# Token means of the first phase by column-tiled float32 products instead of a centring product on every image

## The chip, the cores and the metric

One NeuronCore of a Trainium2 chip runs the whole program. The metric is device time in microseconds (us), the median of several executions. Engines: PE is TensorE, PEld its weight loads, DVE VectorE, ACT ScalarE, POOL GpSimd, SP the engine that issues most DMAs.

## What is computed

The input `x` has 32 images of 128 channels and 56x56 = 3136 tokens. The reference, cut to what matters:

```python
def _ln_c(v, eps=1e-06):
    m = jnp.mean(v, axis=1, keepdims=True)
    s = jnp.var(v, axis=1, keepdims=True)
    return (v - m) / jnp.sqrt(s + eps)

xa = sign_a(x)                # _L0_conv_ref, on _ln_c(x)
wq = quant_weight_W2(w)       # sign of centred, clipped weights, times alpha
y = conv_general_dilated(xa, wq, padding 1, 3x3) + b
mean, var = over (0, 2, 3)    # batch norm over all images
y = relu((y - mean) * rsqrt(var + EPS) * gamma + beta)

x = x + _L0_conv_ref(_ln_c(x), ...)
t = _to_tokens(x)
t = t + _L0_ffn_ref(_ln_t(t), ...)   # router, top half of the tokens, gelu FFN
x = _from_tokens(t, x)
```

Only the sign of the layer-normed input enters the convolution, and the divisor is positive: so the first phase needs sign(x - m), with m the mean over the 128 channels (the partitions) of each token. Batch norm needs the convolution of all 32 images before anything else can go on, hence two phases.

## The kernel before

Channels lie on the 128 partitions, tokens in the free dimension. An image is worked in NCH = 7 chunks of T = 448 tokens (8 rows of 56). **Phase 1** takes each image n through the convolution and stores it as f16 in DRAM (`y_int`); **phase 2** loads x and y again and does the rest (norm, router, search for the threshold, FFN), by tables of positions. The change touches phase 1 alone.

In phase 1 every engine has its own function `phase1(n, b)`, and the next image is made ready while this one is convolved:

- DVE (`split`, L581, and `split_low`, L585): for each chunk of image n+1 a rounded float32r copy `xh` and the rest `xl = x - xh`, into a ring of RING = 4 buffers each. Then `batch_stats` (L605): the statistics of a chunk of y of image n.
- PE (`centre`, L879 and L880): two float32r products of `centre_r` = identity - 1/128 with `xh` and `xl` into one of four PSUM banks: x - m, for one chunk. `newly_due(c)` says which chunks of image n+1 are centred behind which chunk of image n: 2 behind chunks 1, 3, 5 and 1 behind chunk 6. `conv` (L889): nine bf16 products, one for each tap, of a chunk, into one of two PSUM banks; it waits for `y_copied` of two chunks earlier, and for `signed` of its own image, one chunk ahead.
- ACT (`sign`, L479): the sign of the centred bank into the padded bf16 image `sg` (two of them, inside `yo`). L494: y of a chunk from PSUM to `y16`.
- SP: L354 loads image n+2 into `xb[b]` (1568 KB) once image n is split (`split_ready`), L359 stores y of image n (784 KB).

Loops of the engines run two images a turn. In phase 2, `router` (L942) makes a weighted sum over the 128 channels of each token by column-tiled products: 32 output partitions each, four chunks side by side in the four column quarters of the array, then three. The row goes by `wrow` (L753) and DRAM (`w_row`, L390) to `wse` (L395). The gate row comes back from DRAM onto 128 partitions as `gate_all` (L539). The FFN's second product (L986) has float32 operands: four for each chunk.

```python
for i, (w, t) in enumerate(((wsel_h, th), (wsel_h, tl), (wsel_l, th))):
    for q, c in enumerate(chunks):
        last = M(ps[q * COLS:(q + 1) * COLS, T_BANK, 0:T], w[:, COLS - part:2 * COLS - part], cut(t, c),
```

Of the kernel before, what the change touches and what calls it, by code (L numbers as in the profile page):

```python
# [16 lines left out]
C = 128  # L17
# [28 lines left out]
K_ID, K_CEN, K_STRI, K_TRIU, K_ONES, K_CAND, K_CIDX, K_MHALF, K_END = (  # L46
    0, 128, 256, 384, 416, 544, 560, 561, 561 + NT)


def constants():  # L50
# [10 lines left out]
    t[:, K_MHALF:K_END] = -0.5  # L61
# [21 lines left out]
def block_kernel(nc, consts, x_in, cw_in, cb_in, gamma_in, beta_in, wr_in, br_in, w1_in, b1_in,  # L83
# [10 lines left out]
    g_dram = nc.dram_tensor("gate_row", [n_img, TOK], f32).ap()  # L94
    w_dram = nc.dram_tensor("w_row", [n_img, TOK], f32).ap()

    with ExitStack() as ctx:
# [73 lines left out]
        wrow = sb("wrow", [C, T], f32)  # L171
        wse = sb("wse", [C, SLEN], f32)
# [13 lines left out]
        CEN_BANKS, CONV_BANK = (0, 1, 4, 5), 2  # L186
# [24 lines left out]
        x_in_s = [sem(f"x_in{b}") for b in range(2)]  # L211
# [70 lines left out]
        def newly_due(c):  # L282

            return (c - 1, c) if c % 2 else (c,) if c == NCH - 1 else ()

        def ring_free(n, c):

            if c >= RING:
                return n * NCH + c - RING + 1
            return (n - 1) * NCH + (c + RING if c + RING < NCH else c) + 1  # L290
# [28 lines left out]

        MASK_STEPS = 5  # L320
        PART = (slice(0, HALF * T), slice(HALF * T, TOK))
        P1 = (1, n_img - 1)
# [6 lines left out]
        def _(sp):  # L329
# [3 lines left out]
            sp.dma_start(xb[1][:, :], x_v[C:2 * C, :]).then_inc(x_in_s[1], 16)  # L333
            sp.dma_start(w1_f, w1_in).then_inc(params_in, 16)
# [77 lines left out]
        def _(pool):  # L412
# [27 lines left out]
            def phase2(n, b):  # L440
                for pos in range(POS):
                    for m, mb, _ in due(VAR_AT + 1, 1, n, b, pos):
                        pool.wait_ge(var_ready, m + 1)
                        nc.gpsimd.tensor_tensor(rm[:, 0, :], stw[:, 5, :], kt[0:TILE, K_MHALF:K_END],  # L444
                                                ALU.pow).then_inc(rstd_ready, 1)
# [14 lines left out]
        def _(act):  # L460
# [26 lines left out]
            def phase1(n, b):  # L487
                for c in range(NCH):
# [70 lines left out]
        def _(dve):  # L559
# [13 lines left out]
            def split(n, b, c):  # L573

                if is_int(n) and n == 0:
                    if c in (0, HALF):
                        dve.wait_ge(x_in_s[0] if c else x0_begun, 16)
                elif c == 0:
                    dve.wait_ge(x_in_s[b], (n - b) * 8 + 16)
                wait_count(dve, centred, ring_free(n, c))  # L580
                V.tensor_copy(xh[c % RING][:, :], cut(xb[b], c)).then_inc(xh_ready, 1)  # L581

            def split_low(n, b, c):
                dve.wait_ge(xh_ready, n * NCH + c + 1)
                V.tensor_tensor(xl[c % RING][:, :], cut(xb[b], c), xh[c % RING][:, :].bitcast(f32),  # L585
# [12 lines left out]
            for c in range(NCH):  # L598
                split(0, 0, c)
                split_low(0, 0, c)  # L600
# [6 lines left out]
            def phase1(n, b):  # L607
# [18 lines left out]
            phase1(1, 1)  # L626

            dve.wait_ge(squares_summed, 1)
            link(V.tensor_scalar(norms[:, :], ps[:, BC0, 0:2], float(C), 1e-30, ALU.mult, ALU.add))
# [432 lines left out]
```

## Time and profile before

| | us |
|---|---|
| runs: lowest, median, highest of 3 | 2133.52, 2137.33, 2137.93 |
| the profiled execution, its own time | 2127.27 |
| its span in the trace | 2125.5 |
| phase 1, to the end of image 31's convolutions | about 500 |
| PE busy over the span | 1994.1 (94%) |
| DVE, ACT, POOL busy | 1666.4, 1211.1, 933.1 |
| granted TensorE clock, mean | 0.987 |

A program prints the profile. In its rows "L986" is line 986 of the kernel before, "out<-in" are the program's names without buffer numbers, "x1792" is a count, and the text behind "<-" in brackets is what ended the engine's idle time. Records of matmuls overlap, since the array is pipelined: where matters of rate are concerned, starts are compared, not durations.

### The profile page before, as it was taken

To read this page: it belongs to the slowest core of one execution; us is meant where nothing else is said; L and a number is where in the kernel's file an instruction comes from. 1 tells how busy PE (TensorE), PEld (TensorE's weight loads), DVE (VectorE), ACT (ScalarE), POOL (GpSimd) and SP (SyncE) were. 2 spreads that over 40 slices of the span, in tenths; PEclk is the share of its full clock that TensorE was granted. 3 is DMA by queue.
4 is the path that set the end of the run, shared out by engine and by line. 5 is a ranking of instruction groups with operands and counts; after the bars stand their busy time and mean duration, and the time that the engine had idled before them with its cause. 6 is when DMAs were issued, how large, how long until landed. Compare 5 with 4: busy or idle time off the path is not lost. (4 is left out here: it accounts for less than half of the span.)

```text
span 2125.5 us, 35828 instructions
## 1 busy us (share of the span) xinstructions
PE 1994.1 (94%) x9515; PEld 1021.8 (48%) x9515; DVE 1666.4 (78%) x4766; ACT 1211.1 (57%) x2030; POOL 933.1 (44%) x714
## 2 busy tenths in 40 slices
PE   7999999995899999999999999999999999999995
PEld 4555555552444444444444444444444444444442
DVE  6777777775688888877788888888877888888875
ACT  4444444443656566666666666666666656666652
POOL 1000000003455556655556565556655656565543
PEclk9999999997899999999999999999999999999998
DMA  4434344443123332333333333333333333333213
GB/s 163 178 140 181 142 176 154 163 162 111 51 102 122 131 119 111 126 127 112 112 128 117 124 115 124 114 134 111 127 125 112 125 120 129 111 124 124 99 69 124
DMA packets 68726, 267.91 MB, mean 126 GB/s; under 512 B 22352, under 2 KB 27184, under 8 KB 64688
## 3 DMA queue, kind: packets, MB, share of 16 engines
q1 hardware_dynamic: 55264, 214.90, 27.5%
q10 hardware_dynamic: 13392, 52.29, 6.6%
q14 instruction: 52, 0.43, 0.1%
q8 instruction: 18, 0.29, 0.1%
HBM read 188.08 MB, written 77.87 MB: 125 GB/s over the span
## 5 line engine op out<-in xcount | busy, mean ns | idle before, releaser
L986 PE MATMUL ps<-hs,w_c 128*128 128x448 f32 x1792 | 763.7, 553 | 0.6 <-ACT yo L527 0.6
L517 ACT ACTIVATE hs<-ps,b1c,undo 128x448 f32<-128x448 f32 x896 | 609.2, 718 | 127.2 <-PE ps L977 123.4
L986 PEld LDWEIGHTS ps<-hs,w_c 128*128 128x128 f32 x1792 | 313.4, 190 | 208.6 <-issue 176.9
L889 PE MATMUL ps<-yo,cwT 128*128 128x448 bf16 x2016 | 408.7, 355 | 0.0
L430 POOL TENSOR_TENSOR tl<-tr,th 128x448 f16<-128x448 f32 x224 | 244.0, 1090 | 310.5 <-PE ps L977 192.9
L425 POOL TENSOR_TENSOR xb<-xb,zr 128x448 f32<-128x448 f32 x224 | 261.3, 1168 | 269.2 <-ACT zr L545 267.8
L975 PE MATMUL ps<-th,w_h 128*128 128x448 f16 x896 | 319.2, 356 | 19.8 <-ACT hs L517 19.7
L976 PE MATMUL ps<-tl,w_h 128*128 128x448 f16 x896 | 317.1, 354 | 0.0
L977 PE MATMUL ps<-th,w_l 128*128 128x448 f16 x896 | 317.0, 354 | 0.0
L437 POOL TENSOR_TENSOR yo<-yo,base 128x448 f32<-128x448 f32 x224 | 277.7, 1247 | 77.8 <-DVE yo L823 77.8
L527 ACT ACTIVATE yo<-ps,cols 128x448 f32<-128x448 f32 x224 | 141.5, 632 | 241.7 <-PE ps L986 241.4
L889 PEld LDWEIGHTS ps<-yo,cwT 128*128 128x128 bf16 x2016 | 185.9, 97 | 193.5 <-issue 24.3
L494 ACT ACTIVATE y<-ps 128x448 f16<-128x448 f32 x224 | 121.6, 543 | 258.9 <-PE ps L889 258.9
L545 ACT ACTIVATE zr<-y,bn_t,bn_s 128x448 f32<-128x448 f16 x224 | 169.2, 756 | 144.0 <-DMA y<-y_int 128.6
L605 DVE BATCH_NORM_STATS2 base<-y 128x448 f16 (+1 forms) x224 | 140.2, 627 | 118.5 <-ACT y L494 109.0
L729 DVE TENSOR_TENSOR ur<-xb,ps 128x448 f32<-128x448 f32 x224 | 138.5, 618 | 107.5 <-PE ps L966 100.6
L691 DVE BATCH_NORM_STATS2 st<-ps 112x6 f32<-112x128 f32 x896 | 195.1, 282 | 14.3 <-PE ps L931 10.3
L823 DVE TENSOR_TENSOR yo<-yo,gate_all 128x448 f32<-128x448 f32 x224 | 198.0, 887 | 7.9 <-DMA gate_all<-gate_row 7.9
L421 POOL TENSOR_TENSOR sm<-sm,kt 128x1 f32<-128x1 f32 x1 | 0.6, 564 | 452.3 <-DVE sm L679 452.3
L552 ACT ACTIVATE th<-tr 128x448 f16<-128x448 f32 x224 | 129.0, 576 | 106.3 <-DVE tr L738 91.9
L746 DVE SCALAR_TENSOR_TENSOR base<-tr,xb 128x448 f32<-128x448 f32 x224 | 186.7, 834 | 1.2
L444 POOL TENSOR_TENSOR rm<-stw,kt 112x28 f32<-112x28 f32 x32 | 153.5, 4797 | 34.4 <-DVE stw L709 34.4
(132 smaller groups left out, 2324.2 us busy)
## 6 DMA issues: line engine op xcount, KB each, us to landing
xb<-x SPq DMA_DIRECT2D x31, 1568.0 KB, 7.6
xb<-x SPq DMA_DIRECT2D x33, 896.0 KB, 4.5
gate_all<-gate_row ACTq DMA_DIRECT2D x32, 896.0 KB, 4.3
result<-yo SPq DMA_DIRECT2D x32, 896.0 KB, 3.5
y_int<-y SPq DMA_DIRECT2D x32, 784.0 KB, 3.6
xb<-x SPq DMA_DIRECT2D x33, 672.0 KB, 4.3
gate_all<-gate_row ACTq DMA_DIRECT2D x32, 672.0 KB, 5.5
result<-yo SPq DMA_DIRECT2D x32, 672.0 KB, 3.0
```

The lines of the kernel that those rows point to most:

```text
L425: nc.gpsimd.tensor_tensor(cut(xb[b], c), cut(xb[b], c), zr[(b + c) % 2][:, :], ALU.add).then_inc(x1_ready, 1)
L430: nc.gpsimd.tensor_tensor(cut(tl, c), tr[(b + c) % 2][:, :], cut(th, c), ALU.subtract).then_inc(tl_ready, 1)
L437: nc.gpsimd.tensor_tensor(cut(yo[b], c), cut(yo[b], c), cut(base[b], c), ALU.add).then_inc(out_ready, 1)
L517: nc.scalar.activation(hs[(b + slot) % 2][:, j, :], ps[:, H_BANK + j, 0:T], ACT.Gelu_apprx_tanh, bias=b1c[:, j:j + 1], scale=undo[:, 1:2]) ...
L691: last = V.bn_stats(st[:, c * TPG + i, :], ps[0:TILE, BC0 + c % 2, i * C:(i + 1) * C])
L746: V.scalar_tensor_tensor(cut(base[b], c), tr[ring][:, :], 1.0 / T_SCALE, cut(xb[b], c), ALU.mult, ALU.add).then_inc(base_ready, 1)
L823: V.tensor_tensor(cut(yo[b], c), cut(yo[b], c), cut(gate_all, c), ALU.mult).then_inc(gated, 1)
L889: last = M(bank, cwT[:, t, :], sg[b][:, c * ROWS + dy:c * ROWS + dy + ROWS, dx:dx + SIDE], start=t == 0, stop=t == TAPS - 1)
L975: M(bank, w1_h[:, blk], cut(th, c), start=True, stop=False)
L976: M(bank, w1_h[:, blk], cut(tl, c), start=False, stop=False)
L977: M(bank, w1_l[:, blk], cut(th, c), start=False, stop=True).then_inc(h_done, 1)
L986: last = M(bank, w2_c[:, j, :], hs[(b + c) % 2][:, j, :], start=first, stop=final)
```

## The change

- A third x buffer: `xs = [xb[0], xb[1], base[1]]`, image n in `xs[n % 3]`. What lay in `base[1]` (sign and absolute value of the weights, `w1_f`) goes to `th` and `tl`.
- Image 0 keeps the old way. For images 1 to 31, `token_means` on PE makes seven float32 products of a 128x32 stationary tile (one column of 1/128, the others zero) with chunks 0 to 3, then 4 to 6, of x: as in `router`, the four column quarters take a chunk each. For image n+2 it stands behind chunk 1 (`MEAN_SLOT`) of image n's convolution; image 1's stands behind chunk 0 of image 0.
- `copy_mean` on DVE copies the bank to `mrow` (which is `wrow`), behind the third `level` of its image slot. SP writes the seven rows to DRAM (`m_dram`) with two DMAs, waits for them, and reads the row back onto 128 partitions with two DMAs (896 and 672 KB): into `gate_all` for even images, `hs` for odd ones.
- `level` on DVE subtracts the mean in place in x, for one chunk of image n+1 at a time, in place of `split` and `split_low`. ACT takes the sign from there (SBUF), one chunk behind each y copy.
- The loops of PE, DVE and ACT run six images a turn; SP's is written out.
- The table of constants has 64 more columns; the load of image 2 stands ahead of the small parameters.

The diff, cut to its core:

```diff
     t[:, K_CIDX] = np.arange(C) % CAND
-    t[:, K_MHALF:K_END] = -0.5
+    t[:, K_MHALF:K_MSEL] = -0.5
+    t[:, K_MSEL + COLS] = 1.0 / C
     return t
...
 
         cw, cwc = (o[:, TOK - C * TAPS:TOK] for o in yo)
-        cwa = base[1][:, 0:C * TAPS]
-        cws = base[1][:, C * TAPS:C * TAPS * 3 // 2].bitcast(bf16).rearrange("o (t i) -> o t i", i=C)
-        w1_f = base[1][:, 2 * C * TAPS:2 * C * TAPS + HID]
+        cwa = th[:, 0:2 * C * TAPS].bitcast(f32)
+        cws = tl[:, 0:C * TAPS].bitcast(bf16).rearrange("o (t i) -> o t i", i=C)
+        w1_f = tl[:, C * TAPS:C * TAPS + 2 * HID].bitcast(f32)
+        xs = [xb[0], xb[1], base[1]]
...
+        mrow = wrow
...
-        CEN_BANKS, CONV_BANK = (0, 1, 4, 5), 2
+        CEN_BANKS, CONV_BANK, MEAN_BANK = (0, 1, 4, 5), 2, 6
...
+        def mean_part(b, part):
+
+            count = (HALF, NCH - HALF)[part]
+            if b == 0:
+                return gate_all[:, PART[part]]
+            return hs[part][:, 0:count, :].rearrange("p c t -> p (c t)")
+
+        def mean_cut(b, c):
+
+            return hs[c // HALF][:, c % HALF, :] if b else cut(gate_all, c)
...
+        MEAN_SLOT = 1
...
+            sp.dma_start(xs[2][:, :], x_v[2 * C:3 * C, :]).then_inc(x_in_s[2], 16)
...
 
-            def phase1(n, b):
-                sp.wait_ge(split_ready, (n + 1) * NCH)
+            def save_mean(m, b):
+                sp.wait_ge(mean_copied, m)
+                for part in range(2):
+                    count = min(NQ, NCH - part * NQ)
+                    sp.dma_start(m_dram[bass.ds(m, 1), part * NQ * T:(part * NQ + count) * T]
+                                 .rearrange("a (c t) -> (a c) t", t=T),
+                                 mrow[part:part + (count - 1) * COLS + 1:COLS, :]).then_inc(mean_saved, 16)
+                sp.wait_ge(mean_saved, m * 32)
+                if has(m - 2, 1):
+                    sp.wait_ge(levelled, (m - 2) * NCH)
+                for part in range(2):
+                    sp.dma_start(mean_part(b, part), m_dram[bass.ds(m, 1), PART[part]]
+                                 .to_broadcast([C, (HALF, NCH - HALF)[part] * T])).then_inc(mean_in[b][part], 16)
+
+            def phase1(n, i, k):
+                if has(n + 3):
+                    sp.wait_ge(signed, (n + 1) * NCH)
+                    sp.dma_start(xs[i % 3][:, :], x_v[bass.ds((n + 3) * C, C), :]).then_inc(x_in_s[i % 3], 16)
+                elif n + 2 >= n_img:
+                    sp.wait_ge(signed, (n + 1) * NCH)
+                    for part in range(2):
+                        load_x(n + 2 - n_img, n + 2 - n_img, part)
                 if has(n + 2):
-                    sp.dma_start(xb[b][:, :], x_v[bass.ds((n + 2) * C, C), :]).then_inc(x_in_s[b], 16)
-                else:
-                    for part in range(2):
-                        load_x(n + 2 - n_img, b, part)
+                    save_mean(n + 2, i % 2)
                 sp.wait_ge(y_copied, (n + 1) * NCH)
-                sp.dma_start(y_dram[bass.ds(n * C, C), :], y16[b][:, :]).then_inc(y_saved[b], 16)
-
-            pairs(sp, phase1, 1, n_img - 2, 0, n_img)
+                sp.dma_start(y_dram[bass.ds(n * C, C), :], y16[i % 2][:, :]).then_inc(y_saved[i % 2], 16)
+
+            save_mean(1, 1)
+            for n in range(n_img):
+                phase1(n, n % 6, n // 6)
...
-            def sign(n, b, c):
-                g = n * NCH + c
-                act.wait_ge(centred, g + 1)
+            def sign(m, i, c):
+                b = i % 2
+                if is_int(m) and m == 0:
+                    act.wait_ge(centred, c + 1)
+                    z = ps[:, CEN_BANKS[c % RING], 0:T]
+                else:
+                    act.wait_ge(levelled, (m - 1) * NCH + c + 1)
+                    z = cut(xs[i % 3], c)
                 if c == 0:
-                    if has(n - 2):
-                        act.wait_ge(conv_done, (n - 1) * NCH)
-                    if is_int(n) and n < 2:
-                        act.wait_ge(border_clear, n + 1)
-                bank = CEN_BANKS[c % RING]
+                    if has(m - 2):
+                        act.wait_ge(conv_done, (m - 1) * NCH)
+                    if is_int(m) and m < 2:
+                        act.wait_ge(border_clear, m + 1)
                 nc.scalar.activation(sg[b][:, 1 + c * ROWS:1 + (c + 1) * ROWS, 1:1 + SIDE],
-                                     ps[:, bank, 0:T].rearrange("p (r w) -> p r w", w=SIDE),
+                                     z.rearrange("p (r w) -> p r w", w=SIDE),
                                      ACT.Sign).then_inc(signed, 1)
 
             for c in range(RING):
                 sign(0, 0, c)
             nc.scalar.activation(cwa, cwc, ACT.Abs, accum_out=abs_sum).then_inc(abs_summed, 1)
 
-            def phase1(n, b):
+            def phase1(n, i, k):
+                b = i % 2
                 for c in range(NCH):
                     act.wait_ge(conv_done, n * NCH + c + 1)
                     if c == 0 and has(n - 2):
 
                         act.wait_ge(y_saved[b], (n - b) * 8)
                         act.wait_ge(bn_taken, (n - 1) * NCH)
-                    nc.scalar.activation(cut(y16[b], c), ps[:, CONV_BANK + (b + c) % 2, 0:T],
+                    nc.scalar.activation(cut(y16[b], c), ps[:, CONV_BANK + (i + c) % 2, 0:T],
                                          ACT.Copy).then_inc(y_copied, 1)
                     if is_int(n) and n == 0 and c < 2:
-                        for k in (range(RING, NCH - 1), range(NCH - 1, NCH))[c]:
-                            sign(0, 0, k)
+                        for q in (range(RING, NCH - 1), range(NCH - 1, NCH))[c]:
+                            sign(0, 0, q)
                     if has(n + 1):
-                        for k in newly_due(c):
-                            sign(n + 1, 1 - b, k)
-
-            pairs(act, phase1, 3, n_img - 1, 0, n_img)
+                        sign(n + 1, (i + 1) % 6, c)
+
+            sixes(act, phase1, 0, n_img, 1)
...
+            def copy_mean(m, b):
+                dve.wait_ge(mean_done, m)
+                if has(m - 1, 1):
+                    dve.wait_ge(mean_saved, (m - 1) * 32)
+                V.tensor_copy(mrow[:, :], ps[:, MEAN_BANK + b, 0:T]).then_inc(mean_copied, 1)
+
+            def level(m, i, k, c):
+
+                if c in (0, HALF):
+                    dve.wait_ge(mean_in[i % 2][c // HALF], k * 48 + (i + i % 2) * 8)
+                x_c = cut(xs[i % 3], c)
+                V.tensor_tensor(x_c, x_c, mean_cut(i % 2, c), ALU.subtract).then_inc(levelled, 1)
+
+            def phase1(n, i, k):
                 for c in range(NCH):
                     if has(n + 1):
-                        split(n + 1, 1 - b, c)
-                        split_low(n + 1, 1 - b, c)
+                        level(*image_after(1, n, i, k), c)
+                    if c == MEAN_SLOT + 1 and has(n + 2):
+                        copy_mean(n + 2, i % 2)
                     if c:
-                        batch_stats(n, b, c - 1)
+                        batch_stats(n, i % 2, c - 1)
                     elif has(n - 1):
-                        batch_stats(n - 1, 1 - b, NCH - 1)
-
-            phase1(0, 0)
+                        batch_stats(n - 1, (i + 1) % 2, NCH - 1)
...
+            def token_means(m, i, k):
+
+                b = i % 2
+                pe.wait_ge(x_in_s[i % 3], k * 32 + (i // 3) * 16 + 16)
+                if has(m - 2, 1):
+                    pe.wait_ge(mean_copied, m - 2)
+                for part in range(2):
+                    chunks = range(part * NQ, min(NCH, (part + 1) * NQ))
+                    for q, c in enumerate(chunks):
+                        last = M(ps[q * COLS:(q + 1) * COLS, MEAN_BANK + b, 0:T],
+                                 kt[:, K_MSEL + COLS - part:K_MSEL + 2 * COLS - part], cut(xs[i % 3], c),
+                                 start=part == 0, stop=c + NQ >= NCH)
+                last.then_inc(mean_done, 1)
...
+            def phase1(n, i, k):
                 for c in range(NCH):
-                    conv(n, b, c)
+                    conv(n, i % 2, c)
                     if is_int(n) and n == 0 and c < 2:
-                        for k in (range(RING, NCH - 1), range(NCH - 1, NCH))[c]:
-                            centre(0, 0, k)
-                    if has(n + 1):
-                        for k in newly_due(c):
-                            centre(n + 1, 1 - b, k)
-
-            phase1(0, 0)
+                        for q in (range(RING, NCH - 1), range(NCH - 1, NCH))[c]:
+                            centre(q)
+                    if is_int(n) and n == 0 and c == 0:
+                        token_means(1, 1, 0)
+                    if c == MEAN_SLOT and has(n + 2):
+                        token_means(*image_after(2, n, i, k))
+
+            phase1(0, 0, 0)
             pe.wait_ge(squares_ready, 1)
-            M(ps[:, BC0, 0:2], kt[:, K_ONES:K_ONES + C], squares, start=True, stop=True).then_inc(squares_summed, 1)
-            pairs(pe, phase1, *P1, 1, n_img)
+            M(ps[:, T_BANK, 0:2], kt[:, K_ONES:K_ONES + C], squares, start=True, stop=True).then_inc(squares_summed, 1)
+            sixes(pe, phase1, 1, n_img, 2)
```

How this moves instructions. PE, in the loop of phase 1, behind chunk 1 of an image, before: two chunks of the next image are centred there, and again behind chunks 3 and 5.

```order
L889 MATMUL ps<-yo,cwT 128x448 [waits y_copied,signed]
L889 MATMUL ps<-yo,cwT 128x448 x8
L876 ISA
L269 REGISTER_ALU [waits split_ready]
L879 MATMUL ps<-xh,centre_r 128x448 [waits signed]
L880 MATMUL ps<-xl,centre_r 128x448
L876 REGISTER_ALU
```

PE at the same place now, in one of the images ahead of the loop (`ps<-xb,kt` is `token_means`; here it reads image 3):

```order
L965 MATMUL ps<-yo,cwT 128x448 [waits y_copied,signed]
L965 MATMUL ps<-yo,cwT 128x448 x8
L953 MATMUL ps<-xb,kt 32x448 [waits mean_copied,x_in0]
L953 MATMUL ps<-xb,kt 32x448 x6
L965 MATMUL ps<-yo,cwT 128x448 [waits y_copied,signed]
```

The fourteen products with a 128-wide result, two behind every other chunk, have become seven with 32 rows of result, all in one place; no product stands behind chunks 3, 5 and 6 any more.

DVE at the start of phase 1, where image 0 is done in the old way and image 1 waits for its means (`wrow<-ps` is `copy_mean`, `xb<-xb,hs` is `level`):

```order
L632 TENSOR_TENSOR xl<-xb,xh 128x448 [waits xh_ready]
L658 COPY wrow<-ps 128x448 [waits mean_done]
L665 TENSOR_TENSOR xb<-xb,hs 128x448 [waits mean_in1_0]
L665 TENSOR_TENSOR xb<-xb,hs 128x448
L652 BN_STATS base<-y 128x6 [waits y_copied]
L665 TENSOR_TENSOR xb<-xb,hs 128x448
L658 COPY wrow<-ps 128x448 [waits mean_saved,mean_done]
L652 BN_STATS base<-y 128x6 [waits y_copied]
```

Before, image 1's splits stood in this place and waited for nothing but the ring. Now the first `level` waits for the row to go out and come back.

SP, images 0 and 1 of phase 1 now (`L394` loads x, `L381` writes the means, `L388` reads them back, `L402` stores y):

```order
L394 DMA xb<-x 128x3136 [waits signed]
L381 DMA mean_row<-wrow 4x448 [waits mean_copied]
L381 DMA mean_row<-wrow 3x448
L388 DMA gate_all<-mean_row 128x1792 [waits mean_saved]
L388 DMA gate_all<-mean_row 128x1344
L402 DMA y_int<-y 128x3136 [waits y_copied]
L394 DMA xb<-x 128x3136 [waits signed]
L381 DMA mean_row<-wrow 4x448 [waits mean_copied]
```

Before, there stood only the load of x and the store of y for each image. The four DMAs of the means now stand between them, in one queue.

## Rows read from the trace of the kernel before

**Rows 1.** The page: busy time, and the clock granted in 40 slices.

```profile
PE 1994.1 (94%) x9515; PEld 1021.8 (48%) x9515; DVE 1666.4 (78%) x4766; ACT 1211.1 (57%) x2030; POOL 933.1 (44%) x714
...
PEclk9999999997899999999999999999999999999998
```

**Rows 2.** Busy time by stretch: stretch, its length, each engine's busy us, clock, DMA share, GB/s.

```profile
249.80:264.76 14.96, 14.96 (x78) 8.44 (x77) 10.81 (x22) 6.87 (x14) 0.00 (x0) 1.00 0.43 161
264.76:279.72 14.96, 14.96 (x78) 8.44 (x77) 10.90 (x22) 6.87 (x14) 0.00 (x0) 1.00 0.43 161
488.02:500.30 12.28, 12.24 (x64) 6.02 (x63) 8.35 (x8) 4.03 (x9) 0.00 (x0) 1.00 0.53 196
```

**Rows 3.** Groups of instructions from 0 to 560 us: busy us, mean ns | idle before, releaser.

```profile
L889 PE MATMUL ps<-yo,cwT 128*128 128x448 bf16 x2016 | 408.7, 355 | 0.0
...
L605 DVE BATCH_NORM_STATS2 base<-y 128x448 f16 (+1 forms) x224 | 140.2, 627 | 118.5 <-ACT y L494 109.0
L585 DVE TENSOR_TENSOR xl<-xb,xh 128x448 fp32r<-128x448 f32 x224 | 140.1, 626 | 7.7
L494 ACT ACTIVATE y<-ps 128x448 f16<-128x448 f32 x224 | 121.6, 543 | 258.9 <-PE ps L889 258.9
...
L879 PE MATMUL ps<-xh,centre_r 128*128 128x448 f32 x224 | 103.2, 461 | 15.1 <-DVE xl L585 14.7 <-ACT cwT L467 0.4
...
L880 PE MATMUL ps<-xl,centre_r 128*128 128x448 f32 x224 | 82.5, 368 | 0.0
```

**Rows 4.** Timeline of ACT in image 31: start us, length, instruction [idle before].

```profile
491.68 0.54 ACT L494 ACTIVATE y<-ps 128x448 f16<-128x448 f32 x1 [1.18 <-PE ps L889]
...
498.58 0.54 ACT L494 ACTIVATE y<-ps 128x448 f16<-128x448 f32 x1 [1.18 <-PE ps L889]
```

**Rows 5.** The page's groups: the FFN's float32 product in phase 2.

```profile
L986 PE MATMUL ps<-hs,w_c 128*128 128x448 f32 x1792 | 763.7, 553 | 0.6 <-ACT yo L527 0.6
```

**Rows 6.** The chain that ended last: eight of them in a row.

```profile
1539.23 3.01 PE ps L986 x8
```

**Rows 7.** Timeline of PE in phase 2, around the router (L942).

```profile
955.99 0.35 PE L977 MATMUL ps<-th,w_l 128*128 128x448 f16 x1
956.27 0.37 PE L942 MATMUL ps<-th,wsel_h 128*32 128x448 f16 x4
956.48 0.36 PE L942 MATMUL ps<-tl,wsel_h 128*32 128x448 f16 x4
...
957.23 0.36 PE L942 MATMUL ps<-th,wsel_l 128*32 128x448 f16 x3
957.52 0.36 PE L975 MATMUL ps<-th,w_h 128*128 128x448 f16 x1
```

**Rows 8.** Timeline at the start of phase 1, PE.

```profile
23.05 1.90 PE L889 MATMUL ps<-yo,cwT 128*128 128x448 bf16 x9
...
36.81 0.38 PE L917 MATMUL ps<-sm,kt 128*128 128x2 f32 x2
...
37.13 3.62 PE L889 MATMUL ps<-yo,cwT 128*128 128x448 bf16 x18
```

**Rows 9.** Timeline behind the router: the row's way to DRAM and back.

```profile
957.64 0.74 DVE L753 TENSOR_SCALAR wrow<-ps,undo,cols 128x448 f32<-128x448 f32 x1 [0.92 <-PE ps L942]
...
959.00 1.56 SPq L390 DMA_DIRECT2D w_row<-wrow  x2
961.68 0.73 SPq L395 DMA_DIRECT2D wse<-w_row  x1
```

**Rows 10.** The page's DMA issues: count, KB each, median us to landing.

```profile
xb<-x SPq DMA_DIRECT2D x31, 1568.0 KB, 7.6
...
gate_all<-gate_row ACTq DMA_DIRECT2D x32, 896.0 KB, 4.3
...
y_int<-y SPq DMA_DIRECT2D x32, 784.0 KB, 3.6
...
gate_all<-gate_row ACTq DMA_DIRECT2D x32, 672.0 KB, 5.5
```

More of the change, by code:

```diff
@@ L43 @@
 W_TOP = 2.0 ** 14
-K_ID, K_CEN, K_STRI, K_TRIU, K_ONES, K_CAND, K_CIDX, K_MHALF, K_END = (
-    0, 128, 256, 384, 416, 544, 560, 561, 561 + NT)
+K_ID, K_CEN, K_STRI, K_TRIU, K_ONES, K_CAND, K_CIDX, K_MHALF, K_MSEL, K_END = (
+    0, 128, 256, 384, 416, 544, 560, 561, 561 + NT, 561 + NT + 2 * COLS)
 def constants():
@@ L94, in block_kernel @@
     g_dram = nc.dram_tensor("gate_row", [n_img, TOK], f32).ap()
+    m_dram = nc.dram_tensor("mean_row", [n_img, TOK], f32).ap()
     w_dram = nc.dram_tensor("w_row", [n_img, TOK], f32).ap()
@@ L210, in block_kernel @@
         border_clear = sem("border_clear")
-        x_in_s = [sem(f"x_in{b}") for b in range(2)]
+        x_in_s = [sem(f"x_in{b}") for b in range(3)]
+        mean_done = sem("mean_done")
+        mean_copied = sem("mean_copied")
+        mean_saved = sem("mean_saved")
+        mean_in = [[sem(f"mean_in{b}_{part}") for part in range(2)] for b in range(2)]
+        levelled = sem("levelled")
         xh_ready = sem("xh_ready")
@@ L280, in pairs, with sixes, image_after @@
                 body(n, n % 2)
[L282 to L290, printed above, removed]
+        def sixes(eng, body, lo, hi, ahead):
+            first, last = -(-max(lo, 3) // 6), min(hi, n_img - ahead) // 6
+            for n in range(lo, 6 * first):
+                body(n, n % 6, n // 6)
+            with eng.Fori(0, last - first) as t:
+                for i in range(6):
+                    body(t * 6 + (6 * first + i), i, t + first)
+            for n in range(6 * last, hi):
+                body(n, n % 6, n // 6)
+        def image_after(d, n, i, k):
+            return n + d, (i + d) % 6, k + (i + d) // 6
+        def mean_part(b, part):
[5 more added lines that the diff above has]
+            return hs[c // HALF][:, c % HALF, :] if b else cut(gate_all, c)
         def is_int(n):
@@ L318, in done @@
             return (n + shift) * len(steps) + (sum(p < pos for p in steps) - sum(p - POS >= pos for p in steps))
+        MEAN_SLOT = 1
         MASK_STEPS = 5
         PART = (slice(0, HALF * T), slice(HALF * T, TOK))
-        P1 = (1, n_img - 1)
         P2 = (3, n_img - 3)
@@ L443, in phase2 @@
                         pool.wait_ge(var_ready, m + 1)
-                        nc.gpsimd.tensor_tensor(rm[:, 0, :], stw[:, 5, :], kt[0:TILE, K_MHALF:K_END],
+                        nc.gpsimd.tensor_tensor(rm[:, 0, :], stw[:, 5, :], kt[0:TILE, K_MHALF:K_MSEL],
                                                 ALU.pow).then_inc(rstd_ready, 1)
@@ L571, in _, with split, split_low @@
             V.tensor_copy(centre_r[:, :], kt[:, K_CEN:K_CEN + C]).then_inc(tables_ready, 1)
[L573 to L585, printed above, removed]
+            def split(c):
+                if c in (0, HALF):
+                    dve.wait_ge(x_in_s[0] if c else x0_begun, 16)
+                if c >= RING:
+                    dve.wait_ge(centred, c - RING + 1)
+                V.tensor_copy(xh[c % RING][:, :], cut(xb[0], c)).then_inc(xh_ready, 1)
+            def split_low(c):
+                dve.wait_ge(xh_ready, c + 1)
+                V.tensor_tensor(xl[c % RING][:, :], cut(xb[0], c), xh[c % RING][:, :].bitcast(f32),
                                 ALU.subtract).then_inc(split_ready, 1)
@@ L598, in _ @@
             for c in range(NCH):
-                split(0, 0, c)
-                split_low(0, 0, c)
+                split(c)
+                split_low(c)
             def batch_stats(n, b, c):
@@ L624, in _ @@
             V.tensor_reduce(squares[:, 1:2], w1_s[:, :], AX.X, ALU.add).then_inc(squares_ready, 1)
-            phase1(1, 1)
+            phase1(1, 1, 0)
             dve.wait_ge(squares_summed, 1)
-            link(V.tensor_scalar(norms[:, :], ps[:, BC0, 0:2], float(C), 1e-30, ALU.mult, ALU.add))
+            link(V.tensor_scalar(norms[:, :], ps[:, T_BANK, 0:2], float(C), 1e-30, ALU.mult, ALU.add))
             V.tensor_scalar(norms[:, 1:2], norms[:, 1:2], 1.0 / C, None, ALU.mult).then_inc(bound_ready, 1)
-            phase1(2, 0)
+            phase1(2, 2, 0)
             dve.wait_ge(bound_rooted, 1)
@@ L656, in _ @@
             link(V.tensor_tensor(cand0[:, :], neg_b[:, :], candc[:, 0:1], ALU.add))
-            pairs(dve, phase1, 3, n_img - 1, 3, n_img - 1)
+            sixes(dve, phase1, 3, n_img - 1, 2)
             dve.wait_ge(bn_taken, EARLY * NCH)
             V.bn_aggr(bn_early, bnst[:, 0:EARLY * NCH, :])
-            phase1(n_img - 1, (n_img - 1) % 2)
+            phase1(n_img - 1, (n_img - 1) % 6, (n_img - 1) // 6)
             batch_stats(n_img - 1, (n_img - 1) % 2, NCH - 1)
@@ L872, in _, with centre @@
             M = nc.tensor.matmul
-            def centre(n, b, c):
-                g = n * NCH + c
-                pe.wait_ge(split_ready, g + 1)
-                wait_count(pe, signed, ring_free(n, c))
+            def centre(c):
+                pe.wait_ge(split_ready, c + 1)
+                if c >= RING:
+                    pe.wait_ge(signed, c - RING + 1)
                 bank = ps[:, CEN_BANKS[c % RING], 0:T]
@@ L894, in _ @@
             for c in range(2):
-                centre(0, 0, c)
+                centre(c)
             pe.wait_ge(cw_signed, 1)
```

7 lines of the change are left out of this document (4 added, 3 removed).

## The prediction

> **What bounds the kernel now.** I read the page first: PE is busy 94% of the span, at a granted clock of full speed in nearly all slices [rows 1]. Then the busy time by stretch, since the change touches phase 1 alone. In two images from the middle of phase 1 PE is busy for all of the 14.96 us that an image takes; DVE has 10.8, ACT 6.9, and the DMA engines are at 0.43 [rows 2]. So phase 1 goes at the pace of PE's queue, and only what changes there, or what makes PE wait, counts. Third, the groups of instructions, to see what PE does [rows 3]: 2016 convolution products and 224 + 224 centring products, which are 63 and 14 an image. The price of each is read from starts, since records overlap. In image 31, where nothing is centred, four chunks of nine convolution products take 498.58 - 491.68 = 6.90 us [rows 4]: 1.725 a chunk, 12.07 an image. The centring is the rest of an image, 14.96 - 12.07 = 2.89 us, or 0.206 a product.
>
> **What the change takes from PE.** 2.89 us for each of images 1 to 31. The two splits on DVE and their waits go too, which is worth nothing by itself: DVE is not what PE waits for.
>
> **What it puts there: the price of seven float32 products.** No row shows a column-tiled float32 product, so I build it from two. First, a float32 product of 448 columns: phase 2 has 4 x 7 x 32 = 896 of them in the program and the trace shows 1792 [rows 5]: each runs as two instructions. Eight of these follow one another in 3.01 us, 0.376 each, 0.75 a product [rows 6]. Second, the router: four f16 products for four column quarters start as one, and the next group 0.19 to 0.21 later, as one product would [rows 7]. So neighbours in different quarters do run side by side.
>
> In the changed kernel the two halves of one product stand next to each other in the queue, in the *same* quarter; the router writes the quarters innermost and never has this. I take it that PE starts products in the order of the queue. Then the second half of product 1 waits for the first half, and product 2's first half, behind it, starts with it, in the next quarter; and so on: each step overlaps one half with the next product's first half. Seven products make 8 steps of 0.376 = 3.01 us. The router pays 0.28 and 0.29 where its neighbours' stride is 0.19, on entry and exit [rows 7]: 0.19 more. **Together 3.20 us for each image, against 2.89 removed: 0.31 slower.**
>
> The bounds: at the low end all four quarters run at once, two groups of four strides (two halves of two strides), 8 x 0.19 + 0.19 = 1.7 us; at the high end none overlap, 14 x 0.376 + 0.19 = 5.5 us. I take 3.2 because the rows show both of its parts, overlap of neighbours and the two halves; rows 7 carry four f16 streams side by side, which in bytes is two float32 streams, not four.
>
> The Trainium skill, TensorE: Matmul & The Clock Gate (Part 3, The mechanism), says that matmuls start and end in program order, and that only weight loads are pulled ahead. By that rule the eight steps hold; no row here has two halves in one quarter followed by another quarter, so the trace cannot confirm it.
>
> **Where it counts.** `token_means` stands behind chunk 1 in images 0 to 29 (images 2 to 31), and once more in image 0. Image 0 is the start, below. Images 1 to 29: 29 x 0.31 = +9.0 us. Image 30 loses its centring and has no means: -2.9. Image 31 had none.
>
> **The start.** Before, image 1's first splits waited only for the ring, and its convolution starts at 37.13 [rows 8]. Now image 1's means must go to DRAM and back with little to cover them. They start where convolution chunk 1 of image 0 did, at 23.05 [rows 8]; +3.2 for the products; from the end of the router's products (957.52) to the read back (961.68) it is 4.16 us, copy and two writes included [rows 7, 9]; +4.3 until the first 896 KB have landed, as the gate row's [rows 10]; +0.63 for one `level` (same shape and engine as L585 [rows 3]); about 0.55 for the sign and 0.54 for y of chunk 1, queued on ACT behind that sign [rows 3]. That is 36.4. Only then may PE convolve chunk 3 of image 0; with the image's second set of means before it, it stood ready long before. Four chunks, 6.9, end at 43.3. `squares_ready` then comes about 1 us late (DVE's square and sum stand behind the last statistics; before, it was ready at 36.81, in cover of centring). Image 1 starts near 44.4: **+7.3 us**, with 2 either way.
>
> Sum: 7.3 + 9.0 - 2.9 = **+13.4 us**. The profiled execution took 2127.27, so 2140.7; the median shown, 2137.33, is 10 above it, and I carry the difference to the median: 2150.7, say 2151.
>
> **What I cost at nothing, and its cover.** DVE: seven `level` of 0.63, seven statistics of 0.63, a copy of 0.74 [rows 3, 9]: 9.6 of 15.3 us. It now waits for the means at its third place, behind which stand four `level`; they are wanted a whole image later. ACT has as many instructions as before, and reads the sign from SBUF. The transfers of the means: at 3.45 + 3.2 = 6.7 us into the image the products are done; +4.16 is 10.8, when the read back is issued; its 896 KB land at 15.1 and the 672 KB at 16.3 [rows 10]. The first `level` of that image is wanted at 15.3, but ACT's sign must be made only before y of chunk 1 is copied, and PE asks for that copy at its chunk 3, some 8 us into the next image. So there are about 8 us of slack. One thing eats of it: the writes stand in SP's queue behind the load of x and the store of y (7.6 and 3.6 us to landing, issued together at the image's start), but those have landed at about 8.5. The DMA engines move 1568 KB more an image: share 0.43 becomes about 0.7 (0.43 x 14.96 us x 3920/2352 KB, over 15.3 us). The 6-image loops, the larger table and image 2's load ahead of the parameters: under 0.3 us, none on a wait that ends last.
>
> **The rivals.**
> - *All four quarters at once, 1.7 us*: for it speaks that the router's groups do just that. Against it the halves and the order. Steady state 29 x (1.7 - 2.89) = -34.5; the start is 1.5 shorter, +5.8; -2.9. Sum -31.6: **2106**, faster. It decides once the products cost under 2.7 us an image. The Trainium skill's TensorEngine Tiling (Array Packing), Key Properties, calls the tiles independent, each with its own weights and products in parallel. Taken to the letter this gives this rival; the router's rows agree, but they don't test it.
> - *No overlap of float32, 5.5 us*: 29 x 2.6 = +75.4, start +9.6, -2.9, sum +82: **2219**. Against it: the router's overlap. For it: no row has a float32 tile.
> - *The row comes back late*: if the round trip is 8 us longer than I say (writes behind x, 0.7 of the DMA engines in use), PE waits once an image, at its chunk 3. At 1 us an image +29, **2180**. Against it the slack above.
> - *It does less than it says*: products at about 2.9 us, so phase 1 keeps its pace, and only the start and image 30 are left: +4.4, **2142**; the low edge of my own forecast.
>
> **How the numbers follow.** A measurement of this kernel can tell about 0.2%, 4.3 us, from no change. My forecast (products 2.9 to 3.6 us, start 5 to 9) has 0.55 and its own range is 2142 to 2163; a tenth of the whole lies within 4.3 us of no change. All quarters at once: 0.23. No overlap: 0.12. Row late: 0.06. Anything else: 0.04. The range reaches down to the second and up to the fourth, and leaves out no overlap: 2101 to 2180. Faster 0.24, same 0.10, slower 0.66.
>
> **What would show it.** The distance of two convolutions' starts around the means: 3.2 us right, 1.7 or 5.5 the rivals. Product records whose starts lie 0.376 apart in pairs of different quarters. An image period of 15.3 us in the middle, 12.1 in image 30. PE idle between about 31 and 36 us and not again in phase 1; image 1's convolution near 44.4. In the steady state no wait of DVE for the read back that PE then shows. Phase 2 the same as before. I am wrong in the mechanism if the period is under 14.5 or over 16, and wrong in the start if image 1 starts before 42 or after 47.

## The result, and the profile after

The changed kernel takes 2102.19 us (median of 4, 2099.38 to 2103.66) against 2135.43 for the kernel before beside it: a ratio of 0.9856, interval 0.9835 to 0.9877. In another comparison on another chip it was 0.9857 (0.983 to 0.9885), 2096.06 against 2126.86. The forecast was 2151, slower; the result is the rival "all four quarters at once", which stood at 2106.

The page of the changed kernel, its span, its busy times, and the lines on clock and DMA:

```profile
span 2100.1 us, 35007 instructions
...
PE 1961.1 (93%) x9515; PEld 961.7 (46%) x9515; DVE 1600.5 (76%) x4580; ACT 1216.2 (58%) x2030; POOL 938.0 (45%) x714
...
PEclk9999999996999999999999999999999999999998
DMA  6787877852133333333333333333333333333223
```

The number of matmul records is the same as in [rows 1], 9515: fourteen products of one kind gave way to seven that are two records each. The DMA line is near 8 tenths through phase 1, and phase 1 is shorter. Where it ends can be read from the last statistics on DVE. Kernel before, timeline of DVE:

```profile
501.54 0.53 DVE L667 BATCH_NORM_AGGREGATE sm<-base 128x2 f32<-128x84 f32 x1
```

and the changed kernel:

```profile
472.79 0.53 DVE L729 BATCH_NORM_AGGREGATE sm<-base 128x2 f32<-128x84 f32 x1
```

So phase 1 is 28.8 us shorter. From there to the end of the span it is 1624.0 and 1627.3 us. In the traces of all versions here this stretch takes 1614.7 to 1629.5 us, in no order that goes with phase 1: nothing shows that phase 2 was changed.

The busy time in two images from the middle of phase 1, to hold against [rows 2]:

```profile
245.33:259.13 13.80, 13.80 (x80) 6.43 (x78) 8.59 (x15) 7.09 (x14) 0.00 (x0) 1.00 0.77 285
259.13:272.94 13.81, 13.81 (x81) 6.43 (x78) 8.58 (x15) 7.08 (x14) 0.00 (x0) 1.00 0.78 296
```

An image takes 13.80 us instead of 14.96, PE is still busy all the time, DVE's share fell from 10.8 to 8.6 us, and the DMA engines went from 0.43 to 0.77. The timeline of one of these images, PE and then what waits for the means:

```profile
257.49 1.71 PE L953 MATMUL ps<-xb,kt 128*32 128x448 f32 x14
...
259.13 12.24 PE L965 MATMUL ps<-yo,cwT 128*128 128x448 bf16 x63
259.35 0.62 DVE L658 COPY wrow<-ps 128x448 f32<-128x448 f32 x1 [1.50 <-PE ps L953]
...
260.00 1.29 SPq L381 DMA_DIRECT2D mean_row<-wrow  x2
...
262.68 0.81 SPq L388 DMA_DIRECT2D gate_all<-mean_row  x2
```

Fourteen records, from 257.49 to the next convolution at 259.13: **1.64 us, where 3.20 was forecast**. Its weight loads show the form of it:

```profile
257.49 0.16 PEld L953 LDWEIGHTS ps<-xb,kt 128*32 128x32 f32 x8 [0.38 <-issue]
257.90 0.12 PEld L953 LDWEIGHTS ps<-xb,kt 128*32 128x32 f32 x3 [0.25 <-issue]
258.27 0.12 PEld L953 LDWEIGHTS ps<-xb,kt 128*32 128x32 f32 x3 [0.25 <-issue]
```

I read the eight loads in 0.16 us as both halves of four products, one half in use and one ready, in all four quarters. The next loads come 0.41 and 0.78 us after the first, about the stride of a float32 half (0.376 [rows 6]) apart. So there are four strides of 0.376, 1.5 us, and all quarters are at work in each. DVE waits 1.50 us for the products before it copies the means, as forecast, and never for the read back in the steady state; nobody waits for DVE there.

The start, PE:

```profile
28.44 1.71 PE L953 MATMUL ps<-base,kt 128*32 128x448 f32 x14
30.08 1.90 PE L965 MATMUL ps<-yo,cwT 128*128 128x448 bf16 x9
35.85 9.61 PE L965 MATMUL ps<-yo,cwT 128*128 128x448 bf16 x36 [3.88 <-ACT y L544]
46.64 0.38 PE L994 MATMUL ps<-sm,kt 128*128 128x2 f32 x2 [1.17 <-DVE sm L686]
46.88 3.61 PE L965 MATMUL ps<-yo,cwT 128*128 128x448 bf16 x18
```

PE stops for 3.88 us at chunk 3 of image 0 and for 1.17 at the squares, and image 1 starts at 46.88 instead of 37.13 [rows 8]: 9.75 us lost. The 36 convolution products behind the wait take 9.61 us; at full clock they take 6.9 [rows 4]. The stretch shows why:

```profile
35.80:42.00 6.20, 6.15 (x19) 2.57 (x20) 4.27 (x8) 2.72 (x6) 0.00 (x0) 0.57 0.72 264
```

The granted clock is 0.57 there, near the lower of its two levels (1.2 of 2.4 GHz), behind PE's only wait of some length in phase 1.

The sum with the measured prices: start +9.75, 29 images by 13.80 - 14.96 = -1.16, -33.6, image 30 -2.9. That is -26.8, and phase 1 is 28.8 us shorter. Of the 2.0 us that are missing, 1.6 are two waits of PE for the splits in the kernel before, which went with the splits:

```profile
71.42 0.47 PE L879 MATMUL ps<-xh,centre_r 128*128 128x448 f32 x1 [0.75 <-DVE xl L585]
72.91 0.47 PE L879 MATMUL ps<-xh,centre_r 128*128 128x448 f32 x1 [0.82 <-DVE xl L585]
```

The two spans differ by only -25.4, as phase 2 was 3.3 us longer in this execution. That the sum comes near this figure is chance.

### The profile page after: what moved, and what is told of

The parts are those of the page before. It is cut to its first block, busy times and chain, and to the rows that moved or that the text cites. A ratio compares the mean times of both kernels' runs of the same rounds, so it can differ in the third digit from the quotient of the medians.

```text
span 2100.1 us, 35007 instructions
## 1 busy us (share of the span) xinstructions
PE 1961.1 (93%) x9515; PEld 961.7 (46%) x9515; DVE 1600.5 (76%) x4580; ACT 1216.2 (58%) x2030; POOL 938.0 (45%) x714
## 4 chain that ended last, share of the span: by engine, by line
PE 48%; DMA 11%; SPq 6%; DVE 4%; issue 4%; POOL 1%; ACT 1%; ACTq 0%; POOLq 0%; DVEq 0%
PE ps L1063 24%; DMA y<-y_int 6%; PE ps L1052 6%; PE ps L1054 5%; PE ps L1053 5%; PE ps L1008 5%; SPq L429 4%; DMA w_row<-wrow 3%; PE ps L1041 2%; DMA wse<-w_row 2%; SPq L435 1%; POOL rm L489 1%; ACT hs L566 1%; SPq L440 1%; DVE rm L776 1%
## 5 line engine op out<-in xcount | busy, mean ns | idle before, releaser
L965 PE MATMUL ps<-yo,cwT 128*128 128x448 bf16 x2016 | 396.2, 357 | 3.9 <-ACT y L544 3.9
L965 PEld LDWEIGHTS ps<-yo,cwT 128*128 128x128 bf16 x2016 | 193.8, 98 | 214.4 <-issue 24.9
```

Of the source, the lines that this page charges most:

```text
L965: last = M(bank, cwT[:, t, :], sg[b][:, c * ROWS + dy:c * ROWS + dy + ROWS, dx:dx + SIDE], start=t == 0, stop=t == TAPS - 1)
```

## The experiments

After the result, the open question was why float32 products in four quarters cost 1.64 us and not 3.20. Theory A: each column quarter takes its own products as they come, whatever stands between them in PE's queue. Theory B: PE starts products in the order of the queue, and the two halves of a product escape this for another reason. Next: how much of the slack I had claimed for the row is there, and what the start costs.

**The order of the queue.**

```diff
-                for part in range(2):
-                    chunks = range(part * NQ, min(NCH, (part + 1) * NQ))
-                    for q, c in enumerate(chunks):
+                for q in range(NQ):
+                    for part in range(2):
+                        c = part * NQ + q
+                        if c < NCH:
```

> Edit: the seven float32 mean products in another order, all of one quarter's chunks before the next quarter (0, 4, 1, 5, 2, 6, 3 instead of 0, 1, 2, 3, 4, 5, 6). Theory A, each column quarter takes its own products as they come, whatever stands between them in PE's queue: unchanged, 1.64 us an image from the first product to the next convolution, image period 13.80, span 2100. Theory B, PE starts products in the order of its queue, and the two halves of a float32 product don't hold up the next quarter for another reason: the chunks that now stand behind one another in one quarter wait, 11 steps of 0.376 and 0.19, 4.3 us an image, period 16.5, span about 2100 + 29 x 2.7 = 2178.

Measured, one execution: 2102.23 us, beside 2128.36 for the kernel before on the same chip; unchanged against the kernel with the change. In its timeline of PE:

```profile
255.33 1.72 PE L954 MATMUL ps<-xb,kt 128*32 128x448 f32 x14
256.98 12.24 PE L966 MATMUL ps<-yo,cwT 128*128 128x448 bf16 x63
```

1.65 us. Up to four halves of one quarter now stand in a row in the queue, and the next quarter's products behind them are not held up. Theory B in its plain form falls, and with it the premise of the forecast. The Trainium skill, TensorE: Matmul & The Clock Gate (Part 3, The mechanism), says that matmuls start and end in program order. That doesn't fit this run: in that order the second quarter's first half comes behind the fourth half of the first, and 11 strides of 0.376 would be needed. The measurement decides. TensorEngine Tiling (Array Packing), Key Properties, by which tiles operate independently, holds for this run; a run below shows how far.

**One quarter, two quarters.** All seven products in quarter 0, then chunks 0 to 3 in quarter 0 and 4 to 6 in quarter 1, in turns:

```diff
-                    for q, c in enumerate(chunks):
-                        last = M(ps[q * COLS:(q + 1) * COLS, MEAN_BANK + b, 0:T],
+                for c in range(NCH):
+                    last = M(ps[0:COLS, MEAN_BANK + b, 0:T],
+                             kt[:, K_MSEL + COLS - c:K_MSEL + 2 * COLS - c], cut(xs[i % 3], c),
...
+                for part in range(NQ):
+                    for q in range(2):
+                        c = part + NQ * q
```

The copy and the write to DRAM follow the rows (32 and 64 partitions copied instead of 128).

> Edit: all seven mean products in one column quarter, each chunk's mean in a row of its own; the copy takes 32 partitions. Both theories: nothing can overlap, 14 halves of 0.376 and 0.19 are 5.5 us an image, period 17.6, span 2100 + 29 x 3.8 + 5 = 2215 or so. It gives the price of the overlap: if it comes out under 4 us, a half in a 32-wide tile costs less than 0.376.

> Edit: the seven mean products in two column quarters, chunks 0 to 3 in one and 4 to 6 in the other, in turns. If the quarters run side by side however many are in use: 4 groups of two halves, 8 x 0.376 + 0.19 = 3.2 us an image, period 15.4, span 2100 + 29 x 1.56 + 3 = 2148, the slower-than-before value that was predicted for another reason. If two quarters gain nothing over one: 5.5 us, 2215.

Measured, one execution each: 2211.83 and 2138.51 us beside 2128.36 before. The timelines of PE, one quarter:

```profile
260.52 5.45 PE L951 MATMUL ps<-xb,kt 128*32 128x448 f32 x14
265.90 10.32 PE L963 MATMUL ps<-yo,cwT 128*128 128x448 bf16 x53
```

two quarters:

```profile
246.78 3.19 PE L954 MATMUL ps<-xb,kt 128*32 128x448 f32 x14
249.91 12.24 PE L966 MATMUL ps<-yo,cwT 128*128 128x448 bf16 x63
```

5.38, 3.13 and, with four, 1.64 us: 14, 8 and 4 strides of 0.376 and 0.11 to 0.14 besides. A half costs 0.376 in a 32-wide tile as in the full array, and quarters share the time fully, up to four float32 streams at once. Two quarters have exactly the eight strides that I had forecast for four. There an image takes 15.29 us (forecast: 15.3), and image 1 starts at 44.43 (forecast: 44.4):

```profile
44.43 3.61 PE L966 MATMUL ps<-yo,cwT 128*128 128x448 bf16 x18
```

The kernel is slower than before by 10.2 us (forecast: 13.4). Single executions of the kernel before on one chip lie up to 15 us apart, so the traces are the better witness: phase 1 ends 12.0 us later than in the trace before (513.50 against 501.54). So the terms around the price were near, and the price decided the sign: the kernel gains as long as the products cost less than the 2.89 us of the centring minus a share of the start. The start costs 4.5 to 6.9 us more than image 30 gives back, which is 0.15 to 0.24 us for each of the 29 images, so the limit is near 2.7 us.

**How far ahead.** Two quarters again, but the whole first quarter ahead of the second:

```diff
-                for part in range(NQ):
-                    for q in range(2):
+                for q in range(2):
+                    for part in range(NQ):
```

> Edit: as two_quarters, but all four products (eight halves) of the first quarter stand in PE's queue ahead of the three of the second. Theory A, each quarter takes its own products whatever stands between, also this far ahead: 3.13 us an image as in two_quarters, period 15.3, span 2137. Theory B, PE looks only a few products ahead: the second quarter starts late; with the queue in strict order only the eighth half overlaps, 13 x 0.376 and 0.1, 5.0 us an image, span 2137 + 29 x 1.9 = 2192.

Measured: 2160.20 us beside a median of 2124.59 before. Neither theory as it was written. PE's timeline and its weight loads:

```profile
257.53 3.98 PE L954 MATMUL ps<-xb,kt 128*32 128x448 f32 x14
261.44 12.24 PE L966 MATMUL ps<-yo,cwT 128*128 128x448 bf16 x63
```

```profile
257.53 0.14 PEld L954 LDWEIGHTS ps<-xb,kt 128*32 128x32 f32 x2 [0.38 <-issue]
257.93 0.11 PEld L954 LDWEIGHTS ps<-xb,kt 128*32 128x32 f32 x1 [0.27 <-issue]
258.31 0.11 PEld L954 LDWEIGHTS ps<-xb,kt 128*32 128x32 f32 x1 [0.27 <-issue]
258.68 0.11 PEld L954 LDWEIGHTS ps<-xb,kt 128*32 128x32 f32 x1 [0.27 <-issue]
259.06 0.14 PEld L954 LDWEIGHTS ps<-xb,kt 128*32 128x32 f32 x3 [0.27 <-issue]
```

3.91 us, ten strides and 0.15. The first quarter loads a half's weights at each stride, alone, until 259.06; there three loads come at once. The second quarter starts four strides late, when four of the eight halves of the first are done, and its own six then take until stride ten. So independence has a limit. What fits this run and the one with the quarters outermost (where four halves of each quarter are in a row, and nothing is held up): four halves of a quarter, the running one included, can be taken in, and a fifth holds up all that is behind it. It could as well be two whole products; the runs don't tell the two apart. One look-ahead that all quarters share doesn't fit: for a start four strides late it would have to hold five halves, and then the products with the quarters outermost would take six strides or more, where four were measured. The depth is worked out from these two runs and wasn't tried with other lengths.

**The slack of the row.** Products and copy of the means at chunk 3, then at chunk 5 of each image instead of chunk 1:

```diff
-        MEAN_SLOT = 1
+        MEAN_SLOT = 3
...
+        MEAN_SLOT = 5
```

> Edit: MEAN_SLOT 3 instead of 1, so products and copy two chunks (3.45 us) later in each image. The row is read back 3.45 us later too. By the slack of some 8 us that was worked out for the steady state: no wait on PE, period 13.8, span 2100 within 5. Rival, the row comes just in time already: PE waits some us in each image at its chunk 3, +1 us an image is +29.

> Edit: MEAN_SLOT 5, four chunks (6.9 us) later than in the changed kernel. The row would land about 7 us later; by the slack of 8 us it is still just hidden (0 to +1 us an image), by a slack under 6 us PE waits 1 us or more an image, span over 2129.

Measured: 2098.66 and 2204.91 us; the changed kernel on the same chip 2096.06. With chunk 5:

```profile
257.12 0.80 SPq L388 DMA_DIRECT2D gate_all<-mean_row  x2
...
262.08 0.62 DVE L665 TENSOR_TENSOR base<-base,gate_all 128x448 f32<-128x448 f32 x1 [6.86 <-DMA gate_all<-mean_row]
...
262.73 0.58 ACT L528 ACTIVATE yo<-base 128x448 bf16<-128x448 f32 x1 [4.70 <-DVE base L665]
...
263.22 0.53 ACT L544 ACTIVATE y<-ps 128x448 f16<-128x448 f32 x1
...
263.89 1.31 PE L965 MATMUL ps<-yo,cwT 128*128 128x448 bf16 x6 [2.99 <-ACT y L544]
```

This is the chain that the prediction named, `level`, sign, y of chunk 1, convolution of chunk 3, and now PE waits 2.99 us for it in each image. With chunk 3, DVE waits for the row too, 2.9 us, but PE does not:

```profile
259.24 0.62 DVE L665 TENSOR_TENSOR base<-base,hs 128x448 f32<-128x448 f32 x1 [2.90 <-DMA hs<-mean_row]
```

So the move to chunk 3 costs nothing, and the one to chunk 5 makes a wait of 2.99 us. How much slack that means takes one more step. With the products at chunk 1, the 1.64 us of an image's own products stand ahead of its chunk 3 and give the row that much more time; behind chunk 3 or 5 they don't. So the moves take 3.45 + 1.64 = 5.1 us and 6.90 + 1.64 = 8.5 us from the row. 8.5 less the wait of 2.99 is the slack of the changed kernel: about 5.5 us, not 8. With chunk 3 some 0.4 us are left, which fits DVE's wait without one on PE. My figure of 8 left out `level`, sign and copy (1.7 us) and took the image and its products for 3.1 us longer than they are; against this the row is on its way some 2 us sooner. The transfers are not hidden by much.

The wait costs more than itself. The kernel is 109 us slower than the changed one, 3.75 us an image. Most images take 16.9 or 17.0 us, 3.1 to 3.2 more than 13.80, but six take 18.4 to 19.9. The 27 products behind the wait, in one of the former, and in one of the latter with the stretch's busy time and clock:

```profile
246.94 5.33 PE L965 MATMUL ps<-yo,cwT 128*128 128x448 bf16 x27 [2.99 <-ACT y L544]
...
191.67 8.23 PE L965 MATMUL ps<-yo,cwT 128*128 128x448 bf16 x27 [2.94 <-ACT y L544]
...
191.67:197.90 6.23, 6.23 (x18) 2.55 (x19) 4.21 (x8) 2.51 (x5) 0.00 (x0) 0.52 0.93 393
```

Behind this wait of 2.94 us the granted clock was 0.52 over 6.2 us; behind the like one of 2.99 the products ran at full rate.

**The start.** Image 1's products ahead of the transposes of the weights, and the copy on DVE behind the fourth split of image 0:

```diff
             for c in range(2):
                 centre(c)
+            token_means(1, 1, 0)
             pe.wait_ge(cw_signed, 1)
...
-            for c in range(NCH):
+            for c in range(RING):
                 split(c)
                 split_low(c)
...
             copy_mean(1, 1)
+            for c in range(RING, NCH):
+                split(c)
+                split_low(c)
```

> The changed kernel itself, beside the next one: 0.985 of before, span 2100.

> Edit: image 1's mean products ahead of the transposes of the convolution weights, and its copy on DVE behind the fourth split of image 0 instead of behind the seventh. Theory: the start lost 9.7 us (image 1 at 46.88 instead of 37.13), of which about 6 us are PE's wait for image 1's row and 3 us the half clock behind it. The products now cost about 3 us at half clock ahead of image 0, the row is back near 26 instead of 34, and PE doesn't wait: image 1 at 38 to 41, 6 to 9 us less than the changed kernel, clock full throughout. Rival: the wait at the start is hidden later, or the products put ahead delay image 0 by as much: 0 us.

Measured, in five rounds: the changed kernel 2096.06 (2093.94 to 2101.27), this one 2090.34 (2086.75 to 2092.84); 0.9824 of before, interval 0.9797 to 0.9852. PE in its timeline:

```profile
15.07 3.21 PE L956 MATMUL ps<-xb,kt 128*32 128x448 f32 x14
...
30.26 8.79 PE L968 MATMUL ps<-yo,cwT 128*128 128x448 bf16 x45
40.23 0.38 PE L996 MATMUL ps<-sm,kt 128*128 128x2 f32 x2 [1.18 <-DVE sm L689]
40.48 3.61 PE L968 MATMUL ps<-yo,cwT 128*128 128x448 bf16 x18
```

The wait at chunk 3 is gone, and with it the half clock: 45 products in 8.79 us are at full rate. Image 1 starts at 40.48. In the changed kernel it was 46.88, and 44.54 in the trace taken beside this one, where 36 products behind the wait took 8.71 us instead of 9.61: the wait is the same, what the clock adds to it differs from execution to execution. Image 1 starts within the 38 to 41 that were expected. The gain is smaller than the 6 to 9 us expected: 4.1 us at image 1 between the two traces taken side by side, 5.7 between the medians. The changed kernel's start had lost only 7.4 us there, not 9.7. And the clock isn't full throughout: over chunk 0 of image 0 (22.20 to 25.30) the granted clock is 0.50. Last, the product over the squares goes behind image 1:

```diff
-            pe.wait_ge(squares_ready, 1)
-            M(ps[:, T_BANK, 0:2], ...).then_inc(squares_summed, 1)
-            sixes(pe, phase1, 1, n_img, 2)
+            phase1(1, 1, 0)
+            pe.wait_ge(squares_ready, 1)
+            M(ps[:, T_BANK, 0:2], ...).then_inc(squares_summed, 1)
+            sixes(pe, phase1, 2, n_img, 2)
```

> Edit: early_row, and PE's product over the squared weights behind image 1 instead of ahead of it. Theory: PE's wait of 1.2 us for the squares, seen at 40.2 in early_row, goes: image 1 near 39.2 instead of 40.5, 1.2 us less than early_row, which the timing can't tell and the trace can; 0.98 of before. Rival: DVE, which waits for that product behind image 1, is late for image 2 by about as much: 0.

Measured: 2083.53 us (2080.22 to 2085.05) against 2124.59 for the kernel before, 0.9804, interval 0.978 to 0.9828: the lowest ratio here, though its interval overlaps that of the early row alone.

```profile
28.27 1.71 PE L956 MATMUL ps<-base,kt 128*32 128x448 f32 x14
29.91 12.24 PE L968 MATMUL ps<-yo,cwT 128*128 128x448 bf16 x63
42.07 1.71 PE L956 MATMUL ps<-xb,kt 128*32 128x448 f32 x14
```

63 products without a pause are chunks 2 to 6 of image 0 and 0 and 1 of image 1, so image 1 starts at 29.91 + 5 x 1.725 = 38.5, against 37.13 before the change. The wait of 1.2 us is gone. How far it is ahead of the version with the early row alone wasn't timed on one chip; in the traces phase 1 ends 1.8 us earlier (464.58 and 466.38), so what was gained isn't lost again at image 2. Some 0.4 us of it were there before image 1 (29.91 against 30.26 at chunk 2 of image 0), and of the 9.1 us between the two spans 7.3 lie in phase 2, which the edit leaves as it is.

## Why the prediction was wrong

**What bounds: right.** PE was the bound of phase 1 and stayed it; the centring's 2.89 us an image went in full. 29 images of -1.16 are the 2.89 less the products and what stands around them (1.64, and 0.09 of other gaps). One small term was put at nothing: "DVE is not what PE waits for" holds in the steady state, but PE had waited for the splits twice, 1.6 us in all.

**The price of the products: the step that failed.** "I take it that PE starts products in the order of the queue" was the premise, and the eight steps came from it. The runs show quarters that take their work independently, four steps. I had listed this as the low bound and as a rival with 0.23, and gave more to the order because two streams of float32 are the bytes that the router's four f16 streams had shown. Four float32 streams run as well. The router's rows could not tell the cases apart, as the prediction says; to let a rule decide between ends 3.8 us apart, on a term that is multiplied by 29, was the error. The two-quarter run shows the size of it: with 3.13 us the forecast stood, in period, start and sum.

**The start: size off by what it left out.** +7.3 was forecast with products of 3.2 us, which is +5.7 with 1.64. It was +9.75 in the profiled execution and 7.4 in the one beside `early_row`. The wait for the row and the 1.17 us at the squares were as forecast. Missing was the clock: PE's wait of 3.88 us was followed by a stretch at 0.57, and 36 products took 1.8 to 2.7 us longer. Chunk 0 of image 0 was also slower in the profiled execution (3.08 us to the next product instead of 2.15); in the one beside `early_row` it took 2.17, so this isn't the change's doing. It went at about half rate, while the profile's clock row gives 1.00 for that stretch: why is open. In the execution beside `early_row` image 1 starts 7.4 us later than before, against +7.3 forecast. That is luck: the products were taken 1.6 us too dear, and 1.8 us of clock were left out.

**The row's way: the chain right, the slack too large.** From the first convolution behind the products to the read back it is 3.55 us, forecast 4.16; no wait on PE in the steady state, as forecast. The slack is 5.5 us, not 8. The rival "the row comes late" was nearer than its 0.06 said: with the products at chunk 5 it is what happens, with waits of 3 us and 3.75 us an image in all.

**DMA: right.** A share of 0.77 against 0.7 forecast at a longer image (0.78 at 13.8 us), and the load of x lands in 7.4 us as before in 7.6 [rows 10]. DVE's 8.6 us instead of 9.6 forecast: it was no term.

## What to carry to other kernels

Where the sign of a forecast hangs on how two known things combine (here, the halves of a float32 product and column tiles), no row of a kernel that uses them apart decides it; say so in the chances. In this kernel sums over the 128 partitions in 32-wide tiles cost little more than a quarter of what they cost in one quarter (1.64 us against 5.38 for seven of 448 columns), float32 too, as long as the four quarters have work near one another in the queue. And a value that goes through DRAM and back should leave as early as its input allows: the first one has no cover, and an idle PE can pay a second time, in clock.

## What was not expected of the hardware

- Four column tiles stream float32 at once at the full rate: 14 halves in 4 x 0.376 us, 8 and 14 strides in two quarters and one.
- A quarter's products are not held up by those of another quarter ahead of them, up to four halves in a row (1.65 us); with eight in a row the other quarter starts four strides late (3.91 us against 3.13 in turns).
- After 3.88 us without work PE's granted clock was 0.57 over the next 6.2 us, while it was back at work all that time. Behind the wait of 2.9 to 3.2 us that nearly every image has with the products at chunk 5, the clock fell in about one image of five.
